# Second attention: exponentials over three heads instead of two, and TensorE's product written ahead of the scores in two of three steps

## The reference, cut to what matters

```python
attn = jnp.einsum('bhqd,bhkd->bhqk', q, k) * scale + alibi
attn = jnp.where(causal, attn, jnp.finfo(x.dtype).min)
p = jax.nn.softmax(attn, axis=-1)
out = jnp.einsum('bhqk,bhkd->bhqd', p, v)
...
x = x + s * g
```

## Time and profile before

| | us |
|---|---|
| median of 3 runs (lowest, highest) | 874.09 (873.14, 874.2) |
| the profiled execution's time | 875.88 |
| its span in the trace | 874.2 |
| ACT busy | 823.8 (94%) |
| PE busy | 786.2 (90%) |
| PEld busy | 302.1 (35%) |
| DVE busy | 420.2 (48%) |
| POOL busy | 222.9 (25%) |

### The profile page before, as it was taken

One profiled execution on the slowest core, in us unless ns is written; L12 is line 12 of the kernel. 1 busy time (PEld: TensorE's weight loads), 2 busy tenths in 40 slices (PEclk: granted clock), 3 DMA queues, 4 the chain that ended last, 5 costly groups with the idle time before them and its releaser, 6 DMA issues.

```text
span 874.2 us, 21888 instructions
## 1 busy us (share of the span) xinstructions
PE 786.2 (90%) x9230; PEld 302.1 (35%) x9230; DVE 420.2 (48%) x892; ACT 823.8 (94%) x917; POOL 222.9 (25%) x268
## 2 busy tenths in 40 slices
PE   3869999899999999999999999997988978988986
PEld 2422433234343433433343433223333323323322
DVE  7931265473657652677537588996021121121122
ACT  7679999999999999999999996769999999999996
POOL 5301110130212041111303021203334334334333
PEclk9969999999999999999999999998999999999999
DMA  6793020100210300203000016100203112022000
GB/s 189 285 283 58 2 78 3 61 18 2 78 51 1 127 2 23 82 25 115 13 3 25 26 45 210 39 25 1 67 13 90 41 50 90 15 77 90 13 1 25
DMA packets 31947, 53.43 MB, mean 61 GB/s; under 512 B 5480, under 2 KB 16360, under 8 KB 31848
## 3 DMA queue, kind: packets, MB, share of 16 engines
q1 hardware_dynamic: 31848, 52.01, 18.9%
HBM read 31.29 MB, written 20.71 MB: 59 GB/s over the span
## 4 chain that ended last, share of the span: by engine, by line
PE 73%; ACT 17%; DVE 4%; issue 4%; DMA 1%; PEldq 0%; PEld 0%; SPq 0%; ACTq 0%; DVEq 0%
PE c_ps L1263 27%; PE c_ps L1246 13%; ACT c_ring L1966 11%; PE c_ps L112 10%; PE c_ps L2159 8%; PE c_ps L2120 8%; ACT c_ring L1003 3%; PE c_ps L615 1%; PE c_ps L1681 1%; DVE early L1626 1%; PE c_ps L1696 1%; ACT xs L1973 1%; PE c_ps L1688 1%; ACT c_ring L1484 1%; PE c_ps L606 1%
## 5 line engine op out<-in xcount | busy, mean ns | idle before, releaser
L1003 ACT ACTIVATE c_ring<-c_ps 128x1024 f32<-128x1024 f32 x512 | 473.3, 1033 | 4.2 <-PEq L1227 2.9
L1263 PE MATMUL c_ps<-c_ring,vt 128*18 128x256 f32 (+1 forms) x3072 | 271.6, 456 | 0.0
L1966 ACT ACTIVATE c_ring<-c_ps 128x1024 f32<-128x1024 f32 x288 | 267.4, 1070 | 1.1 <-PE c_ps L2120 0.7
L2159 PE MATMUL c_ps<-c_ring,vt 128*18 128x512 f32 (+3 forms) x1664 | 152.5, 468 | 2.0 <-issue 0.9
L1246 PE MATMUL c_ps<-q_st,k_st 32*128 32x512 f32 x1016 | 129.5, 498 | 19.9 <-ACT c_ring L1003 18.9
L1991 POOL TENSOR_SCALAR_AFFINE_SELECT c_ring<-c_ring 128x512 f32<-128x512 f32 x128 | 84.5, 679 | 173.6 <-ACT c_ring L1966 173.1
L1263 PEld LDWEIGHTS c_ps<-c_ring,vt 128*18 128x18 f32 x3072 | 64.9, 97 | 142.5 <-issue 102.5
L2120 PE MATMUL c_ps<-q_st,k_st 32*128 32x512 f32 (+3 forms) x768 | 80.0, 416 | 34.0 <-ACT c_ring L1966 30.2
L1246 PEld LDWEIGHTS c_ps<-q_st,k_st 32*128 32x128 f32 x1016 | 49.8, 182 | 135.4 <-ACT c_ring L1003 132.5
L1024 POOL TENSOR_TENSOR early<-early 128x512 f32<-128x512 f32 x32 | 38.4, 1201 | 176.3 <-DVE early L1147 176.3
L2120 PEld LDWEIGHTS c_ps<-q_st,k_st 32*128 32x128 f32 x768 | 39.8, 185 | 108.2 <-ACT c_ring L1966 99.0
(11 more groups left out here) (248 smaller groups left out, 776.3 us busy)
## 6 DMA issues: line engine op xcount, KB each, us to landing
q_st<-q_hl SPq DMA_DIRECT2D x48, 256.0 KB
k_st<-k_hl SPq DMA_DIRECT2D x48, 256.0 KB
q_hl<-parts SPq DMA_DIRECT2D x10, 512.0 KB, 4.4
k_hl<-parts SPq DMA_DIRECT2D x10, 512.0 KB, 4.7
q_hl<-c_ring SPq DMA_DIRECT2D x4, 512.0 KB, 3.7
k_hl<-c_ring SPq DMA_DIRECT2D x4, 512.0 KB, 4.4
out_dram<-x SPq DMA_DIRECT2D x7, 256.0 KB, 4.2
x<-in_L_attn_x_dram SPq DMA_DIRECT2D x3, 512.0 KB, 5.7
```

Of the source, the lines that this page charges most:

```text
L1003: nc.scalar.activation(probs[t % RING][:, 2 * pair:2 * pair + 2, :], scores[unit % SLOTS][:, :, :], ACT.Exp).then_inc(expd, 1)
L1263: ins = nc.tensor.matmul(o_ps[32 * h:32 * h + 2 * W9, c0:c1], vt[b % 2][:, kt, gp, h, W9 * gs:W9 * gs + 2 * W9], probs[t % RING][:, h, c0: ...
L1966: nc.scalar.activation(probs[t % RING][:, first:first + 2, :], scores[unit % SLOTS][:, :, :], ACT.Exp).then_inc(expd, 1)
L2159: ins = nc.tensor.matmul(o_ps[32 * h:32 * h + 2 * W9, q0:q0 + w], vt[b % 2][:, kt, gp, h, W9 * gs:W9 * gs + 2 * W9], probs[t % RING][:, h, ...
```

## The change

A unit of exponentials is now three heads (1536 columns, three banks) instead of two, so three steps have four units, and a unit may take heads of two neighbouring steps. The scores have two slots of three banks instead of three slots of two; the output bank and the side bank are the two others. The ring holds 18 tiles (four and a half steps) instead of 16, so a step's four tiles can lie around its end, and then GpSimd masks each block in two instructions. LAG1 is 3. TensorE's list is written over three steps: in step t with t % 3 = 0 scores, fill, product; in the two others product, scores, fill; the fourth unit of scores stands at the end of the third step. Products are no longer split. The clearing of the output bank moves behind a VectorE step of the coupling net, the third exponential waits for `twisted[0]` and the sixth for `twisted[1]`, and two buffers move to the end of the ring's allocation.

```diff
-LAG1 = 2
+LAG1 = 3
+TILES = 18
+WIDE = 3
+def last_unit(t):
+    return (G * t + G - 1) // WIDE
+def spans(t):
+    first = G * t % TILES
+    if first + G <= TILES:
+        return [(first, first + G)]
+    return [(first, TILES), (0, first + G - TILES)]
...
     def act_part(act):
+        for u in range(UNITS):
+            first, last = WIDE * u // G, (WIDE * u + WIDE - 1) // G
+            if u == 2:
+                act.wait_ge(twisted[0], 2 * CYCLES)
+            if u == TILES // WIDE - 1:
+                act.wait_ge(twisted[1], 2 * CYCLES)
+            if WIDE * u >= TILES:
+                act.wait_ge(pv_done, (WIDE * u + WIDE - 1 - TILES) // G + 1)
+            act.wait_ge(scored, u + 1)
+            at = WIDE * u % TILES
+            nc.scalar.activation(probs[:, at:at + WIDE, :], wide[u % 2], ACT.Exp).then_inc(expd, 1)
...
     def pool_part(pool):
...
-                part = probs[t % RING][:, :, n * P:(n + 1) * P]
+                for first, last in spans(t):
+                    part = probs[:, first:last, n * P:(n + 1) * P]
...
     def pe_part(pe):
+        def score(u):
+            if u >= 2:
+                pe.wait_ge(expd, u - 1)
...
+            for t in range(WIDE * u // G, (WIDE * u + WIDE - 1) // G + 1):
...
+                places = [at for at in range(G) if (G * t + at) // WIDE == u]
+                banks = {order[at]: wide[u % 2][:, (G * t + at) % WIDE, :] for at in places}
...
+                for n, (gs, kt, q0, at, w) in enumerate(pieces):
+                    for i in banks:
...
+            ins.then_inc(scored, 1)
...
-        for pair in range(LAST):
-            even, odd = 2 * pair, 2 * pair + 1
...
+        for t in range(S + LAG1):
+            if t >= LAG1 and t % 3 != 0:
+                product(t - LAG1)
+            if t < S:
+                score(4 * (t // 3) + t % 3)
+            for one in pieces_at(t // 2) if t % 2 == 0 else ():
+                piece_of(*one)
+            if t >= LAG1 and t % 3 == 0:
+                product(t - LAG1)
+            if t < S and t % 3 == 2:
+                score(4 * (t // 3) + 3)
...
-        ring = sb("ring", [P, RING * G, HALF])
+        ring = sb("ring", [P, RING * G + 4, HALF])
```

## The result

The changed kernel takes 930.3 us (median of 4 runs, 929.31 to 934.63), against 873.62 (873.04 to 874.2) for the kernel before: 1.0658 times as long, 95% interval 1.0628 to 1.0688. Forecast were 917 us, between 896 and 931. The direction and the main mechanism were right; one cost of some 20 us, TensorE's clock, was missing altogether, and the other terms together were 7 us too high. Three single runs stand far off the others of their kernel, two at a lower granted clock (891.21 us in experiment 4, 977.88 in experiment 11) and one of before beside experiments 1 to 4 (1745.96 us); ratios and ranges leave them out, but for the ratio of experiment 4.

The account below looks back on a forecast made before the run. ScalarE bounded the kernel before; after the change TensorE's chain of 282.2 us plus units, caps, fills, transposes, masks and start made 314.9 against 271.2, some 43 us more: 917 us, range 896 to 931.

Parts of the forecast that it names:

- The chain: Second attention, one exponential's end to the fourth after: TensorE's links sum to 5.88 us per cycle, 282.2 over 48.
- own range: Forecast case, chance 0.62: 908 to 925 us, from masks and caps without their waits to a wide exponential of 1.53.
- the rival of the masks: GpSimd's 256-column selects cost as much as 512-column ones, so masks become the bound: 930 us, chance 0.10.
- Units across two steps: Unit 4n + 6: the next step's head starts only behind second pieces, 0.32 us each, 24 times, 7.7.
- The rival of heads side by side: The next step's head runs beside the others in separate row groups: 906 us, chance 0.20.
- The transpose: Products of r = 5 and 23 wait for VectorE's transpose: 0.56 us, 8 times, 4.5.
- Caps: Two capped middle steps per batch lengthen the chain by 1.01 us, 8 times, 8.1 in all.
- Fills: Fills at scores 4n + 4 or behind 4n + 5 delay the chain by 0.43 us, 16 times, 6.9.
- split masks: Steps around the ring's end: products wait 0.36 us for GpSimd's four selects, 13 times, 4.7 in all.
- the start: Start and end of the stretch: 1.5 us for VectorE's last step, less 0.5 and 0.25, together +0.8.
- The waits of TensorE: TensorE waits some 0.9 us before each cycle's fourth unit and the next's first, none before second and third.
- ScalarE's idle time: ScalarE idles some 45 us ahead of the 192 exponentials, ended by the scores.

Follow-up runs that it names:

- experiment 4: Changed kernel with every product behind the scores and VectorE's transpose behind r = 17 ahead of the gate: 878.88 us, ratio 1.0095.
- experiment 11: Changed kernel with that transpose ahead of the gate and an extra 512-column product ahead of every fourth unit's scores: 913.08 us, ratio 1.0444.
- Runs 3: Changed kernel with every product behind the scores in all three steps, transpose not moved: 884.7 us, ratio 1.0108.
- run 1: Changed kernel with VectorE's output-bank transpose behind r = 17 (and 35) one place earlier, ahead of the gate: 927.82 us, ratio 1.0594.
- Run 2: Changed kernel with every fourth unit's scores made twice, same output: 918.95 us, ratio 1.0507.
- run 9: Changed kernel with the product ahead of the scores in one step of three only, and the transpose ahead of the gate: 890.53 us, ratio 1.019.
- run 12: Changed kernel with the transpose ahead of the gate and an extra 256-column product ahead of every fourth unit's scores: 912.91 us, ratio 1.0451.
- experiment 5: Changed kernel with every fourth unit's scores made three times: 923.95 us, ratio 1.0573.
- runs 2, 5 and 8: The last, 8: changed kernel with every fourth unit's scores made twice and the transpose ahead of the gate: 915.86 us, ratio 1.0473.
- run 10: Experiment 4's kernel with another order (scores, product, scores, fills, scores, product, scores, product) in three cycles per batch: 886.93 us, ratio 1.0143.

## Why the prediction was off, step by step

- **The chain: right.** 5.82 per plain cycle against 5.88, link by link as above. A run of three wide exponentials takes 4.13 with one of 1.45, so 1.34 from start to start and 1.45 alone, as forecast. Runs 3 and 4 confirm that the order is the cause: with every product behind scores most of the waits go.
- **The missing step: the granted clock.** Each duration of the sum was read where the clock was at its upper level ("at a granted clock of 1.00 ... in the steady stretches"), and the same text had TensorE standing still ahead of units 4n + 7 and 4n + 8. The step that failed is that the idle time which the sum gives TensorE was taken to leave those durations as they were. It cost 22 of the 59 us in the profiled execution. 930.3 us is outside the forecast's own range, 908 to 925; that it still lies inside the wide one is luck: its upper end, 931, was set by the rival of the masks, and the terms that were 7 us too high made up for a part of the clock. Run 11 shows the clock's cost by itself: the same lists and waits as in run 1 and a product more per cycle, no falls, 17 us less. Run 2 (more work, less time) and the 20 us of busy time between run 9 and the changed kernel, for the same matmuls, say the same. The Trainium skill, TensorE: Matmul & The Clock Gate, section "A second HAM failure mode: psum-queue depth-cycling", tells of a kernel whose TensorE idles briefly between groups of matmuls, often enough for the clock to swing between its levels. The trace agrees: TensorE's longest single wait in the steady part is 1.5 us, and the clock fell twelve times.
- **Units across two steps: mis-sized.** 0.32 each, 7.7 in all, measured 0. The rival of heads side by side held in this, by the row at 686.51, though not in the capped cycles, where the next head starts only behind the second cap of its unit (786.58 in the trace). Had it been taken, the forecast would have been lower, and further off.
- **The rival of the masks: not what happened.** It named 930, the measured time, but for another reason: it priced a select of 256 columns at the 0.61 of one of 512. It takes 0.41, as forecast (0.40):

```profile
L2010 POOL TENSOR_SCALAR_AFFINE_SELECT c_ring<-c_ring 128x256 f32<-128x256 f32 x64 | 23.7, 406 | 13.1 <-ACT c_ring L1983 13.1
```

- **The gate: missed.** 4.1 us, by run 1. The transpose was costed at 0.56 as waiting for the product alone (rows show 0.50, as at 692.36 in the changed kernel), and it was not looked up what stands ahead of it in VectorE's list after LAG1 moved it.
- **Caps: right.** 6.86 for a capped cycle, 1.04 over a plain one, forecast 1.01. **Fills, transposes and split masks** come together to what was forecast within a microsecond: without clock the stretch is 6.9 under the forecast, of which the chain is 2.9, the straddling units are 7.7 and the gate gives back 4.1; the 0.4 left is all that these terms and the start can be off together. The single terms were not taken apart, so errors among them may cancel.
- **The waits of TensorE** were said to be 0.9 ahead of both the fourth unit and the first of the next cycle; they are 0.19 and 0.91. ScalarE's idle time, forecast at 45 us, is 59.0, which has the clock's 22 in it.

In all: +36.8 us by waits, forecast 43.7, and +22.3 by the clock, forecast nothing.

**What stays open.** Where exactly a fall comes was not foretold. Every cycle of the changed kernel has three units of scores with no product between them, and only some have a fall. A product put there ends the falls (run 11); half a product (run 12) and copies of the scores (runs 2, 5 and 8) do so only in part, so whether the kind of work or its amount decides is not shown. In runs 1 and 8 some falls turned up in new places when the wait behind the gate was gone, and the one of run 10 stands behind a stretch in which TensorE was busy for nine tenths of the time. No order tried with wide exponentials beat the kernel before.

## What to carry to other kernels

A sum of links is only as good as the clock at which its durations were read: where it gives TensorE new stretches with little work on a chain that TensorE bounds, add a case in which the granted clock falls there, priced from rows at the lower level (here two products of 1.9 us became 3.3, and a fall cost 1.5 us and more). A run with useless matmuls on top is a cheap test: here it was faster, and the rows showed the clock higher. And where a constant such as a lag moves one engine's instructions, read what now stands ahead of them in that engine's list: a transpose that slipped behind a gate cost 4.1 us, and only the order of VectorE's list would have told.

## What the runs showed of the hardware that was not expected

- Redundant matmuls made the kernel faster: 11 us with 200 more of scores (918.95 for 930.3), 14.7 us with a product more per cycle (913.08 for 927.82), with fewer falls or none, while no cycle at the full clock got shorter.
- The clock fell without any long pause: twelve times in the changed kernel, where no wait of TensorE in the steady part is longer than 1.5 us, and in experiment 5 behind scores and caps without a pause (759.05). Small changes move the falls: in experiment 1 the ninth cycle of every batch was slowed (7.6 to 7.7 us), in the changed kernel not one of them (6.64).
- Two heads in two pieces and a head of another step, five matmuls in three row groups, ended within 0.51 us of their first start: a row group's second piece did not hold up a later head of another group, which started ahead of it.
